# A graph network layer on one core: weights merged by two engines, maxima through TensorE, normalised rows kept in memory, and a changed order at the last edge group

## What is computed

```python
xn = layernorm(x)
support = segment_sum(edge_weight[:, None] * xn[src], dst)          # gather, weigh, add
x = x + support @ gnn_weight + gnn_bias + linear_attention(xn)      # 8 heads, elu(t) + 1
z = layernorm(x)
gh = relu(z @ gfc1_w.T + gfc1_b)                                    # the gate
g  = (gh @ gfc2_w.T + gfc2_b).mean(rows)                            # 8 numbers
W1m = W1 + sum_e g[e] * tv_W1[e];  b1m = b1 + g @ tv_b1             # 256 x 512, merged weights
W2m = W2 + sum_e g[e] * tv_W2[e];  b2m = b2 + g @ tv_b2             # 512 x 256
res = z + relu(z @ W1m.T + b1m) @ W2m.T + b2m
x = x + (res - mean(res)) * rsqrt(var(res) + eps) * lng + lnb
```

## Time and profile before

| | |
|---|---|
| median of three runs | 1876.7 us |
| the profiled execution | 1881.32 us, its span 1879.5 us |
| busy share of the span | TensorE 82%, VectorE 64%, GpSimd 49%, ScalarE 37% |
| mean granted TensorE clock | 0.93 |
| DMA | 353.64 MB, 188 GB/s; the fullest 47 us move 324 GB/s at a busy share of 0.92 |

### The profile page before, as it was taken

How to read it: one execution, slowest core, us unless ns; L and a number is a source line. 1 busy time by engine, 2 the same in 40 slices (tenths; PEclk the granted TensorE clock), 3 DMA queues, 4 the chain that set the end, 5 groups by cost and what they waited for, 6 DMA issues and landing times.

```text
span 1879.5 us, 27602 instructions
## 1 busy us (share of the span) xinstructions
PE 1549.2 (82%) x8551; PEld 672.3 (36%) x8551; DVE 1212.1 (64%) x2230; ACT 702.8 (37%) x1098; POOL 919.1 (49%) x919
## 2 busy tenths in 40 slices
PE   0699968888988898787888888888887799888883
PEld 0345423333333333243333333333333444453331
DVE  7888734554544555456776777676667666468996
ACT  3266522222222232212332333333333677425554
POOL 3000056666666666646666666666663000016776
PEclk9799989999999999978999999999999799989996
DMA  5389777777777777746666666666665422333332
GB/s 182 127 297 324 272 238 227 220 214 224 225 227 223 227 225 225 213 123 193 194 197 200 196 195 196 195 196 197 196 197 154 159 78 79 115 115 107 134 134 83
DMA packets 149271, 353.64 MB, mean 188 GB/s; under 512 B 24773, under 2 KB 30551, under 8 KB 149155
## 3 DMA queue, kind: packets, MB, share of 16 engines
q0 software_dynamic: 62720, 205.57, 37.0%
q1 hardware_dynamic: 84926, 145.42, 22.6%
q10 hardware_dynamic: 1509, 1.21, 0.2%
HBM read 287.93 MB, written 65.38 MB: 188 GB/s over the span
## 4 chain that ended last, share of the span: by engine, by line
PE 37%; DVE 18%; another core or an unknown queue 16%; issue 14%; ACT 9%; DMA 2%; DVEq 1%; ACTq 0%; SPq 0%; POOL 0%; POOLq 0%
PE bank L1550 26%; PE bank L1659 4%; PE bank L1633 4%; ACT mb L642 2%; PE bank L1649 2%; DVE acc L1164 2%; ACT part L636 2%; DVE st L1058 1%; PE bank L1592 1%; ACT qT L663 1%; DVE res L1511 1%; DVE zr L1539 1%; DVE zl L1092 1%; ACT zh L598 1%
## 5 line engine op out<-in xcount | busy, mean ns | idle before, releaser
L850 POOL DMA_INDIRECT rows<-y_rows,idxT x784 | 767.9, 979 | 613.3 <-issue 395.1
L1164 DVE SCALAR_TENSOR_TENSOR acc<-bank,maskt,acc 128x512 f32 x392 | 275.4, 744 | 200.3 <-remote 107.4
L642 ACT ACTIVATE mb<-bank,ones,ncols 128x512 f32<-128x512 f32 x98 | 76.6, 782 | 527.5 <-remote 290.6
L1550 PE MATMUL bank<-KVP,qT 128*128 128x512 f16 x588 | 168.2, 446 | 72.1 <-ACT qT L663 62.1
L1649 PE MATMUL bank<-rows,hots 128*32 128x512 f16 x2352 | 194.3, 402 | 38.7 <-issue 35.1
L1659 PE MATMUL bank<-part,plc 128*128 128x512 f32 x392 | 212.1, 622 | 12.3 <-ACT part L636 6.0
L636 ACT COPY part<-bank 128x512 f32<-128x512 f32 x196 | 113.0, 577 | 192.7 <-remote 145.5
L1550 PE MATMUL bank<-Wg,xtb 128*128 128x512 f16 x588 | 143.3, 396 | 25.6 <-DVE xtb L1103 25.5
L1550 PE MATMUL bank<-Wk,xta 128*128 128x512 f16 x588 | 142.9, 394 | 1.2 <-issue 1.0
L1633 PE MATMUL bank<-xr,kh 128*128 128x512 f16 x392 | 124.8, 402 | 16.7 <-DVE kl L1191 13.4
L1649 PEld LDWEIGHTS bank<-rows,hots 128*32 128x32 f16 x2352 | 78.1, 143 | 166.4 <-issue 144.3
(11 more groups left out here) (278 smaller groups left out, 2324.0 us busy)
## 6 DMA issues: line engine op xcount, KB each, us to landing
xta<-xt_rows SPq DMA_DIRECT2D x98, 256.0 KB
x_rows<-xhl SPq DMA_DIRECT2D x49, 256.0 KB, 2.6
xt_rows<-xtb SPq DMA_DIRECT2D x49, 256.0 KB, 3.0
y_rows<-yb SPq DMA_DIRECT2D x49, 256.0 KB, 2.5
rows<-y_rows,idxT POOLq DMA_INDIRECT x784
xr<-x_rows SPq DMA_DIRECT2D x49, 256.0 KB
zt_rows<-ztg SPq DMA_DIRECT2D x49, 256.0 KB, 2.0
acc<-in_x SPq DMA_DIRECT2D x48, 256.0 KB, 3.1
```

The costliest lines, as they stand in the source:

```text
L642: nc.scalar.activation(mb[:, :], of[:, :], ACT.Relu, scale=ncols[:, col:col + 1], bias=ones[:, 0:1]).then_inc(f_min, 1)
L850: pool.indirect_dma_start(out=rows[:, slot].rearrange("p a d -> p (a d)"), out_offset=None, in_=y_rows, in_offset=bass.IndirectOffsetOnAxi ...
L1164: nc.vector.scalar_tensor_tensor(out=flat(acc, tile + m), in0=placed_bank(s)[:, :], scalar=maskt[:, m, s:s + 1], in1=flat(acc, tile + m), ...
L1550: ins = nc.tensor.matmul(dest, lhs, rhs, start=(n == 0 and only), stop=(n == len(pairs) - 1), skip_group_check=not only)
```

## The change

1. **Edge groups.** `graw` is loaded during the query tiles, measured by VectorE at slot 107 (`gate_largest`), reduced over partitions by GpSimd at slot 113 between gathers, and its scale made at slot 117. In slot 195 the order on TensorE is now `place(194)`, `mix(48)`, `part(195)`. `EDGE_BANKS` is rotated so that `graw` can be turned into banks 2, 3, 5 and 4 before the last groups are added.
2. **Norm and gate stage.** The table load of ScalarE's square root and the high part of `G16` come ahead of the wait for the last edges. SyncE also stores `zn` of each tile, f32, 256 KB, to the new `z_rows`; ScalarE waits for the store of two tiles back. The loads of W1, W2, `tvW1` and the first pair of `tvW2` are spread over ticks 0 to 7 and 40 to 42 in place of one burst ahead of the first tick. GpSimd adds `lnbb` to `acc` here, from the tick at which `lnbb` is made.
3. **Merge.** ScalarE makes the `geye`. Of W1, experts 4 to 7 are merged by TensorE (a product with `geye` turns and adds) and 0 to 3 by VectorE; of W2, 6, 7, 0, 1 by TensorE and 2 to 5 by VectorE. Maxima go through TensorE: a transpose, VectorE's reduce, and a product of ones with a diagonal. The split of b2 moves to GpSimd, the high part of W2m to ScalarE.
4. **Output stage.** `zq` is loaded from `z_rows`, one tile at a time, two tiles ahead, once `res` has freed its buffer. `res` also writes its row sum; VectorE makes the negative mean, ScalarE squares the deviations with a row sum (`squares`). Five tiles behind, VectorE makes `cen` = (res - mean) * lngb and `ob` = cen / deviation + acc. GpSimd has no work here.

```diff
@@ slot 195, TensorE
-                part(s)
+                if s != NGR - 1:
+                    part(s)
+                else:
+                    place(s - 1)
                 t = tile_of(q_slot, s - 4)
                 if t is not None:
                     mix(t)
...
-                place(s - 1)
+                if s != NGR - 1:
+                    place(s - 1)
+                else:
+                    part(s)
@@ norm and gate stage, SyncE
             def tail_stores(g, j):
+                if exists(g, j):
+                    t, b = tile_at(g, j), j % 2
+                    sp.wait_ge(tail.high, 2 * t + 1)
+                    waited(sp)
+                    at_least(sp, z_kept[b], 16 * half_at(g, j))
+                    waited(sp)
+                    sp.dma_start(row_tile(z_rows, t), zn[:, b, :]).then_inc(z_kept[b], 16)
+                if isinstance(g, int):
+                    load_weights(tile_at(g, j))
@@ norm and gate stage, GpSimd (the additions were in out_tick)
+            pool.wait_ge(ln_out, 2)
+            def tail_tick(g, j):
+                if exists(g, j):
+                    t = tile_at(g, j)
+                    pool.wait_ge(tail.high, 2 * t + 2)
+                    waited(pool)
+                    pool.tensor_tensor(flat(acc, t), flat(acc, t), lnbb[:, :], ALU.add).then_inc(based, 1)
@@ merge, TensorE
+            for n, e in enumerate(W1_TURNED):
+                pe.wait_ge(eye_made, n + 1)
+                for f in range(C):
+                    for m in range(FC):
+                        nc.tensor.matmul(bank[f // 2][...], tvW1[:, e, m, f * P:(f + 1) * P], geye[:, e, :], ...)
+            pe.wait_ge(w1_merged, NE - len(W1_TURNED))
...
+            hidden(0, 0, Q4 * P, [0])
+            turn_max(2, 5, 5)
+            hidden(0, 0, Q4 * P, [1])
+            spread_max(2, 2)
@@ output stage, SyncE
+                if exists(gn, jn) and exists(g, j):
+                    sp.wait_ge(res_made, tile_at(g, j) + 1)
+                    waited(sp)
+                    load_z(tile_at(gn, jn), j % 2)
@@ output stage, VectorE
                     nc.vector.scalar_tensor_tensor(out=res[:, j, :], in0=bank[4 + b][:, :], scalar=cols[:, 4:5],
-                                                   in1=zq[:, b, :], op0=ALU.mult, op1=ALU.add).then_inc(res_made, 1)
-                    nc.vector.bn_stats(st6[:, j % Q4, :], res[:, j, :]).then_inc(six_made, 1)
+                                                   in1=zq[:, b, :], op0=ALU.mult, op1=ALU.add,
+                                                   accum_out=rsum[:, j // Q4, j % Q4:j % Q4 + 1]).then_inc(res_made, 1)
...
+                    nc.vector.scalar_tensor_tensor(out=cen[:, :], in0=res[:, j5, :], scalar=negm[:, par5, i5:i5 + 1],
+                                                   in1=lngb[:, :], op0=ALU.add, op1=ALU.mult).then_inc(gained, 1)
...
+                    nc.vector.scalar_tensor_tensor(out=ob[:, b5, :], in0=cen[:, :], scalar=rsr[:, par5, i5:i5 + 1],
+                                                   in1=flat(acc, t5), op0=ALU.mult, op1=ALU.add).then_inc(ob_made, 1)
...
-                    nc.vector.tensor_tensor(zr[:, b, :], zr[:, b, :], lngb[:, :], ALU.mult).then_inc(gained, 1)
@@ output stage, ScalarE
-                    next_input(gn, jn)
+                    nc.scalar.activation(squares[:, :], res[:, j1, :], ACT.Square, bias=negm[:, par, i:i + 1],
+                                         accum_out=dev2[:, par, i:i + 1]).then_inc(squared, 1)
```

More of the change, by code:

```diff
@@ L705, in gate_weights @@
                 for f in range(C):
-                    nc.scalar.activation(G16[:, 0, f, :], bank[2 + f][:, :], ACT.Copy, scale=scf[:, 0:1]
+                    nc.scalar.activation(G16[:, 0, f, :], bank[GATE_BANKS[f]][:, :], ACT.Copy, scale=scf[:, 0:1]
                                          ).then_inc(high_made, 1)
@@ new lines, in out_tick @@
+                g1, j1 = back(g, j, 1)
+                if exists(g1, j1):
+                    t, par, i = tile_at(g1, j1), j1 // Q4, j1 % Q4
+                    act.wait_ge(mean_made, t + 1)
+                    at_least(act, squared, t)
+                    waited(act)
+                    nc.scalar.activation(squares[:, :], res[:, j1, :], ACT.Square, bias=negm[:, par, i:i + 1],
+                                         accum_out=dev2[:, par, i:i + 1]).then_inc(squared, 1)
+                if j % Q4 == 0 and not (isinstance(quad, int) and quad == 0):
+                    last = isinstance(quad, int) and quad == NQ
+                    n = 1 if last else Q4
+                    act.wait_ge(squared, T if last else Q4 * quad)
+                    at_least(act, r_scale, quad - 1)
+                    nc.scalar.activation(sd4[:, 0:n], dev2[:, (j // Q4 + 1) % 2, 0:n], ACT.Sqrt, scale=1.0 / D,
+                                         bias=epsx[:, :]).then_inc(r_std, 1)
@@ L1526, in out_tick @@
                                [j % Q4 - 1])
[L1527 to L1541 removed]
+            row_ticks(dve, out_tick, T + OUT_LAG)
         @block.tensor
@@ new lines, in _, with turn_max @@
+            pe.wait_ge(w1_merged, NE - len(W1_TURNED))
+            for f in range(C):
+                for m in range(FC):
+                    ins = nc.tensor.matmul(bank[f // 2][:, (f % 2) * F + m * P:(f % 2) * F + (m + 1) * P],
+                                           W1raw[:, m, f * P:(f + 1) * P], ident[:, :], start=False, stop=True,
+                                           skip_group_check=True)
+            ins.then_inc(w1_done, 1)
+            def turn_max(n, first, made):
+                pe.wait_ge(maxes_made, made)
+                nc.tensor.transpose(bank[6][0:n, 0:P], mx[:, first:first + n], ident[:, :]).then_inc(max_turned, 1)
@@ new lines, in spread_max, with add_turned @@
+            def spread_max(n, count):
+                pe.wait_ge(max_row, count + 2)
+                nc.tensor.matmul(bank[6][:, P:P + n], ones[0:n, :], maxdiag[0:n, 0:n], start=True, stop=True
+                                 ).then_inc(max_turned, 1)
+            def add_turned(e, first):
+                pe.wait_ge(eye_made, NE)
+                for o in range(FC):
+                    for c in range(C):
+                        nc.tensor.matmul(bank[4 + o][:, c * P:(c + 1) * P], tvW2[:, e, c, o * P:(o + 1) * P],
+                                         geye[:, e, :], start=first and c == 0, stop=False, skip_group_check=True)
```

357 lines of the change are left out of this document (204 added, 153 removed).

## The result

The changed kernel takes 1859.8 us, the median of four runs, against 1878.4 for the kernel before beside it: ratio 0.990, 95% interval 0.986 to 0.994. The profiled execution took 1863.5 us (span 1861.6) against 1881.3. The forecast was 1854.7 with a range of 1839 to 1870, from a median of 1876.7 for the kernel before: right in direction and in what bounds each stage, 5 us too hopeful in size.

A forecast was written before the change was run, and what follows sets the result against it. TensorE was taken to bound the norm and gate stage, VectorE the output stage. The terms sum to -22.0 us: 1859.3 from the profiled 1881.3, or 1854.7 against the median, range 1839 to 1870.

The forecast's parts named there:

- The output loop: Output stage, first to last `res`: 12.8 us a quad, 153.6 for twelve in place of 176.8, -23.2 us.
- I add 0.7 us a quad for that: Output stage: allowance for TensorE waiting for `xd` loads, now issued after the wait for the quad's first `res`.
- The norm stage: Norm and gate stage: GpSimd's 49 additions and the `zn` stores cost +6 us, ends 0 and +12.
- The hold once a quad: Norm stage: GpSimd's addition holds VectorE's bias operation by some 0.25 us a quad, 3 us over 12 quads.
- Merge: Merge of W1 and W2: W2m finished and next hidden product started at 1674.4 against 1676.08, -1.7 us, ends -6 and +2.
- The measuring of `graw`: Edge groups, slot 107: its 2.25 us on VectorE delays queued work, +0.5 us, ends 0 and +3.
- 2: Norm stage: GpSimd's addition takes the lock ahead of `zl`, +24 us in all, 1901 us; chance in full 0.05.
- its one-in-four case: Norm stage: `zl` loses to GpSimd in one tick a quad, 13 us in place of 6, 1862; within the forecast's 0.68.
- 3: Output stage: `cen` and `ob` take twice as long, 205 us in place of 153.6, 1906 us; chance 0.03.
- 5: Output stage: the square needs another table than the square root, two loads a quad on ScalarE, 1860; within the forecast's 0.68.
- 4: Output stage: the `z` load is late at every tile, 1878 us; chance 0.04.
- 1: Output stage: VectorE or the loads stay the bound, quad 14 us, loop -8.8 in place of -23.2, 1869; chance 0.20.

The follow-up runs named there:

- Experiment 1: Kernel before with GpSimd's additions of `lnbb` left out of the output stage: 1693.6 us against 1727.1, ratio 0.982.
- paced: Changed kernel with each GpSimd addition of `lnbb` released seven tiles later: 1695.1 us, 1.9 under the unaltered changed kernel.
- experiment 3: Changed kernel with GpSimd's additions of `lnbb` left out of the norm and gate stage: 1700.3 us, ratio 0.984 to the kernel before.
- experiment 4: Changed kernel without the `z` stores and the waits on them, loading rows of `x` instead: 1698.6 us, ratio 0.984 to the kernel before.
- experiment 7: Changed kernel with the spreading of the W2 maxima ahead of the second half of the hidden product: 1698.2 us against 1697.0 unaltered.
- third set: Kernels run together on the chip where the kernel before takes 1880 us; the changed kernel took 1862.7 us there, ratio 0.990.

## Why the prediction was right, and where it was off

**The output loop**: forecast -23.2 (153.6 us), measured -19.2 in the pair (157.6), -22.7 by the mean of seven executions (154.1 against 176.8). The causes were right: TensorE's 12.06 is the bound, and `xd` is late. VectorE's quad was put too high at 11.5 to 12.1: the durations do add up to 11.5, but an operation starts some 0.07 us before the one ahead of it has ended, and VectorE is busy for 114.2 us of the stage, 9.5 a quad. Even so its low part `hT` came late at times, a wait that the prediction had at nothing. The term mis-sized was "I add 0.7 us a quad for that": in the profiled execution the waits for `xd` were 10.2 + 2.2 = 12.4 us, 1.0 a quad; over the seven executions they are 0.7. It also left out the clock behind a pause, which made 4.45 us of 2.75 once in this profile. But the step that named the reason was only half an argument: I took 2.8 us a quad of statistics (4 x 0.694) away as part of the gain. Experiment 1 shows that with the lock gone TensorE is the bound even with the statistics kept.

**The norm stage**: forecast +6 (0 to 12), measured +9.5 in the pair; over all executions 166.0 on the mean of the five with the changed norm stage against 159.2 of the three with the old one, +6.8. The backlog was put at 3 us and is worth 2.8 (166.0 to 163.2 when paced). The hold once a quad was put at 3 and is worth some 2 (163.2 to 161.0 with no additions), but the step that named its place was wrong: behind the backlog `nb` lasts 0.16 us in every quad but the last (0.25). What is held is `rs`, the operation ahead of it, 405 ns in place of 168, or 0.24 a quad; by the prediction's rule of two SBUF inputs it was free (experiment 3). What is left, 161.0 and 161.9 against 158.4 to 159.8, is about 2 us that neither GpSimd nor, by experiment 4, clearly the stores explain; it stays open.

**Stage start** -1: measured -1.8. **Merge** -1.7: measured -1.5 for the product behind W2m (40.5 in place of 42.0 us from the gate's end), and the reason for so small a gain was the one given: W1 is turned 7.9 us earlier, and most of it is lost behind W2 and behind the half hidden product (experiment 7). At the first `res` only 0.6 of it is left, since the product behind W2m took 5.00 us in place of 4.14. **End** -2 (its sum, 6 x 1.6 + 2, is 11.6 and not 11.7): measured -3.0. **Slot 195**: measured about -0.8 against -0.6. **The measuring of `graw`** in slot 107: 2.28 us on VectorE at 913.7, with no loss that the stage's end shows. The 2.9 us gained by then are within scatter: in four profiles of kernels whose edge groups are those of the changed one, on chips of this kind, the first `zl` starts at 1449.4, 1451.6, 1455.6 and 1457.8.

**Luck.** The total is closer than its terms. In the pair the loop, the norm stage and the merge are together 8.6 us worse than forecast (4.0, 3.5 and 1.1), and 4.6 came back in the edge groups (2.8, scatter), at the end (1.0) and at the stage's start (0.8).

**The rivals.** 2 falls, its one-in-four case too: `zl` starts 0.11 us ahead of GpSimd and lasts 0.69, and behind the first 30 us of the stage none lasts longer. 3 falls, and with it the rule of the Trainium skill (Vector Engine (DVE) Microarchitecture Reference, Points that are easy to get wrong) as far as this form goes: `cen` and `ob` at 741 and 751 ns for 512 columns of two f32 tensors in SBUF are as quick as `res` with one of them in a bank. 5 falls: ScalarE's table loads stay at four in the whole kernel and none lies in the output stage. 4 falls: `res` waited for `zq` once, 0.3 us. 1 came in part: `xd` was late, but the mean quad is 157.6 / 12 = 13.1 us and not 14.

## What to carry to other kernels

Where GpSimd and VectorE both work on SBUF tensors, look first for a tiny VectorE operation as long as a GpSimd one: here moving one addition of 1.3 us a tile was worth the output stage's gain, and rewriting VectorE's arithmetic showed none of its own. Check one-input operations too: `rs` and `sc` were held. Moving such work into another stage needs its release paced, or what has piled up runs as one block. A load that is issued behind a wait for something unrelated in the same queue should be moved ahead as soon as its buffer is free; where it makes TensorE pause, the lower clock behind it can cost nearly as much again (1.7 us behind 2.1 here), though it did so behind four of twelve such pauses only.

## What was not expected of the hardware

The same kernel takes 1727 to 1731 us on two chips and 1880 on a third. The stages from the first gate product on are alike; the 150 us lie in the edge groups: the first gather starts at 240 to 244 us in all profiles, and the first gate product starts at 1475.2 in the kernel before on the slow chip and at 1317.6 in experiment 1, whose edge groups are the same. The changed kernel, 600 to 900 us into its span, on the third set's chip and on the second's:

```profile
600.00:900.00 300.00, 259.31 (x1352) 104.88 (x1350) 167.33 (x311) 77.53 (x124) 187.12 (x194) 0.92 0.70 208
```
```profile
600.00:900.00 300.00, 276.35 (x1610) 116.33 (x1611) 211.28 (x391) 95.76 (x151) 226.72 (x227) 0.98 0.76 234
```

1352 products against 1610, gathers 194 against 227, clock 0.92 against 0.98. The gathers' times say more. A gather usually starts 1.25 us after the one before, in all profiles. In the six profiles of 1847 to 1892 us, 97 to 100 of the 784 gathers start more than 2.2 us after the one before, about one in eight and always between two groups of edges, 303 to 314 us in all; in the eight of 1685 to 1704 us 2 to 4 do, 11 to 23 us. Less the usual step these pauses are 180 to 190 us against 9 to 18, enough for the 150. TensorE also stands 56 to 88 us there without a wait that the profile shows, against 2 or less. What makes the engines pause is not known, nor whether the lower clock follows from it. Whatever the cause, the change's gain holds on both kinds, 0.990 and 0.982.

The row sum written along with a VectorE operation is an instruction of its own of 83 ns, but the operation behind it starts at the same moment (`cen` and the row sum both at 1786.35), so it held nothing up there.
